# Routed expert tokens in 8 expert lists instead of 28 pair lists, with tiles of 512 rows stored split and loaded transposed

## The reference

```
x = x + conv_part(layernorm over channels(x))
    # conv_part: per image and channel a 3x3 depthwise convolution whose 9 taps are a softmax of
    # linear maps of the channel means and maxima, plus a bias, plus its own input
t = tokens(x)                                # 32768 tokens of 128 channels
n = layernorm(t)
logits = n @ Wg + bg                         # 8 experts
top 2 of the 8, weights = softmax over the 2
t = t + sum over the 2 chosen e of  w_e * (gelu(n @ W1[e] + b1[e]) @ W2[e] + b2[e])     # H = 512
return images(t)
```

## Time and profile before

| | |
|---|---|
| median of 3 runs | 1804.54 us (1803.85 to 1805.2) |
| span of the profiled execution | 1798.2 us |
| TensorE busy | 1536.5 us, 85% |
| VectorE busy | 1396.4 us, 78% |
| ScalarE busy | 1202.0 us, 67% |
| GpSimd busy | 866.1 us, 48% |
| moved by DMA | 115.76 MB |

### The profile page before, as it was taken

How to read it: one execution, slowest core, us unless ns; L and a number is a source line. 1 busy time by engine, 2 the same in 40 slices (tenths; PEclk the granted TensorE clock), 3 DMA queues, 4 the chain that set the end, 5 groups by cost and what they waited for, 6 DMA issues and landing times.

```text
span 1798.2 us, 45758 instructions
## 1 busy us (share of the span) xinstructions
PE 1536.5 (85%) x12335; PEld 1186.0 (66%) x12336; DVE 1396.4 (78%) x2440; ACT 1202.0 (67%) x2949; POOL 866.1 (48%) x905
## 2 busy tenths in 40 slices
PE   5889999999999519999999999999999999999665
PEld 2445555555555307878888778878777788878555
DVE  0468888788788737888888888888888888888644
ACT  3466667767666308878777887788777887888400
POOL 1003455355355464555555555555555555555500
PEclk8899999999998659999999999999999999999965
DMA  3211121121121061111111111111111111110099
GB/s 120 59 35 56 54 72 59 59 70 60 61 58 49 31 146 30 39 39 36 42 42 37 36 38 39 39 40 35 41 42 37 40 38 42 42 37 22 22 374 359
DMA packets 90626, 115.76 MB, mean 64 GB/s; under 512 B 15286, under 2 KB 71794, under 8 KB 90583
## 3 DMA queue, kind: packets, MB, share of 16 engines
q1 hardware_dynamic: 65784, 62.29, 12.2%
q0 software_dynamic: 18176, 34.27, 5.5%
q10 hardware_dynamic: 6624, 18.69, 2.8%
HBM read 60.22 MB, written 58.61 MB: 66 GB/s over the span
## 4 chain that ended last, share of the span: by engine, by line
issue 31%; POOL 28%; PE 24%; ACT 7%; DMA 4%; DVE 4%; POOLq 1%; SPq 0%; ACTq 0%; DVEq 0%
POOL token_out L454 12%; POOL yt L449 9%; PE psV L731 8%; POOL yt L447 6%; DMA ye<-token_out 4%; PE psR L703 3%; PE psV L691 3%; ACT spent L531 2%; PE psA L682 2%; PE psT L716 2%; PE psR L747 2%; PE psG L718 1%; POOL rows_by_pair L439 1%; DVE x L963 1%; ACT sq L508 1%
## 5 line engine op out<-in xcount | busy, mean ns | idle before, releaser
L1138 DVE TENSOR_TENSOR gl<-g,gh 128x1024 f16<-128x1024 f32 x312 | 438.1, 1404 | 70.5 <-ACT gh L624 65.2
L439 POOL DMA_INDIRECT rows_by_pair<-rows,idx x256 | 265.0, 1035 | 393.3 <-issue 245.4
L454 POOL DMA_INDIRECT token_out<-yt,rt x312 | 323.1, 1036 | 184.6 <-POOL yt L449 133.5
L616 ACT ACTIVATE g<-psV,b1col 128x256 f32<-128x256 f32 x624 | 244.4, 474 | 143.6 <-PE psV L825 143.6
L616 ACT ACTIVATE g<-psT,b1col 128x256 f32<-128x256 f32 x624 | 244.4, 474 | 53.4 <-PE psT L825 53.4
L731 PE MATMUL psV<-lp,diag 128*128 128x512 f32 x512 | 254.2, 626 | 24.8 <-ACT cv L524 14.6
L823 PE MATMUL psV<-xh,wall 128*128 128x256 f16 x624 | 171.9, 275 | 94.6 <-DVE xl L1128 53.8
L447 POOL TENSOR_TENSOR yt<-ya 128x256 f32<-128x256 f32 x156 | 112.9, 724 | 247.0 <-DVE ya L1150 246.9
L841 PE MATMUL psG<-wall,gh 128*128 x1248 | 222.7, 273 | 1.7 <-DVE ya L1146 1.4
L841 PE MATMUL psR<-wall,gh 128*128 x1248 | 222.7, 273 | 0.7 <-DVE ya L1150 0.7
L842 PE MATMUL psG<-wall,gl 128*128 x1248 | 214.3, 219 | 0.0
(11 more groups left out here) (187 smaller groups left out, 3254.9 us busy)
## 6 DMA issues: line engine op xcount, KB each, us to landing
rt<-rows_by_pair SPq DMA_DIRECT2D x156, 133.0 KB, 2.1
xb<-in_x_dram SPq DMA_DIRECT2D x32, 512.0 KB, 3.5
ye<-token_out SPq DMA_DIRECT2D x32, 512.0 KB, 9.1
out_dram<-oe ACTq DMA_DIRECT2D x32, 512.0 KB, 5.8
token_out<-yt,rt POOLq DMA_INDIRECT x312, 2.3
rows_by_pair<-rows,idx POOLq DMA_INDIRECT x256, 2.4
stage<-in_L_ffn_W_dram SPq DMA_DIRECT2D x1, 2048.0 KB, 12.3
rows_by_pair<-pad_rows SPq DMA_DIRECT2D x15, 133.0 KB, 5.2
```

What stands on the lines that cost most here:

```text
L439: gp.indirect_dma_start(rows_dram, bass.IndirectOffsetOnAxis(ap=idx[p][:, b:b + 1].bitcast(U32), axis=0), rows[p][:, b, :], None).then_inc ...
L454: gp.indirect_dma_start(y_dram, bass.IndirectOffsetOnAxis(ap=rt[r][:, b, ID:ID + 1].bitcast(U32), axis=0), yt[r][:, b, :], None, bounds_ch ...
L616: last = sc_.activation(g[side][:, s * T:(s + 1) * T], hbank[side][:, s * T:(s + 1) * T], ACT.Gelu, bias=b1col[:, bass.ds(e * HS + s, 1)], ...
L1138: v.tensor_tensor(gl[side][:, :], g[side][:, :], gh[side][:, :], ALU.subtract).then_inc(lo_done, 1)
```

## The change

- **Lists.** Each token goes to two of 8 lists, one for each chosen expert. The indicator has 8 columns. The second entry of a token comes from a second buffer, `twin`, into which a DMA on SP's queue copies the row. GpSimd writes 32 times 128 rows in a unit. A row has 130 words: the token, its target row and its weight.
- **Split and normalised in stage A.** ScalarE normalises a token when it is turned (8 activations for an image, in place of the one copy in `keep`) and rounds it to float16, and VectorE forms the low part. The rows are stored as float16 high and low parts.
- **The convolution's result** is stored in HBM by SP for the last addition, which moves to stage C.
- **Tiles** have 512 rows of one expert: 136 tiles, in a ring of four. SP loads them transposed, so there is neither normalising, turning nor splitting in stage B; target rows and weights come with a second small load.
- **Stage B.** The up product has 512 columns. The gelu, casts and rests are made slice by slice (two casts on ScalarE, two on VectorE). The down product is as before for one expert, over four blocks of 128 rows, two PSUM banks to a tile, two sets of banks in turn. ScalarE copies the side columns of the bank to SBUF, VectorE adds them to the others and multiplies by the weight. GpSimd only issues four indirect stores, to one row for each choice of a token.
- **Stage C** loads both choices of each image and the convolution's result (16 images of it are loaded at the start of stage B), turns both on TensorE and adds the three on VectorE.

The diff, cut to its core:

```diff
-    T = 2 * P
+    T = 4 * P
     TB = T // P
-    CAP = NTOK + 2 * T
-    OFF = [a * (2 * E - a - 1) // 2 for a in range(E - 1)]
-    NT = NTOK // T + NPAIR
+    CAP = NTOK + T
+    NT = 2 * NTOK // T + E
...
-    RING = 6
-    assert NT % RING == 0 and RING % 6 == 0
+    RING = 4
+    assert NT % RING == 0
...
+            def copy_rows(st_, stage, k):
+
+                p, blks = st_.slot(stage), slice(k * NBLK, (k + 1) * NBLK)
+                sp.wait_ge(low_ready, st_.count(stage, 2, k + 1))
+                sp.dma_start(twin[p][:, blks, 0:2 * XW], rows[p][:, blks, 0:2 * XW]).then_inc(twin_in[2 * p + k], 16)
...
             def load_rows(first, r):
-                sp.dma_start(rt[r][:, :, :], rows_dram[bass.ds(first, T), :].rearrange("(p b) f -> p b f", b=TB)).then_inc(row_in[r], 16)
+                src = rows_dram[bass.ds(first, T), :]
+                sp.dma_start_transpose(xt[r][:, :, :], src[:, 0:2 * XW].bitcast(F16)).then_inc(row_in[r], 16)
+                sp.dma_start(meta[r][:, :, :], src[:, ID:RW].rearrange("(b p) f -> p b f", p=P)).then_inc(row_in[r], 16)
...
+            for j in range(NX):
+                load_x1(j, j)
+
...
+            def load_e(n, j):
+                for k in range(2):
+                    src = y_v[n] if isinstance(n, int) else y_v[bass.ds(n, 1)].rearrange("a p k b d -> (a p) k b d")
+                    sp.dma_start(ye[j][:, k, :, :], src[:, k, :, :]).then_inc(ye_in[j], 16)
...
-                    for b in range(NB2):
-                        gp.indirect_dma_start(rows_dram, bass.IndirectOffsetOnAxis(ap=idx[p][:, b:b + 1].bitcast(U32), axis=0),
-                                              rows[p][:, b, :], None).then_inc(rows_out[2 * p + b // NBLK], 16)
+                    pool.wait_ge(low_ready, images)
+                    for k in range(2):
+                        for c, src in enumerate((rows[p], twin[p])):
+                            if c == 1:
+                                pool.wait_ge(s_const, 3)
+                                pool.wait_ge(twin_in[2 * p + k], copies)
+                            for b in range(k * NBLK, (k + 1) * NBLK):
+                                gp.indirect_dma_start(rows_dram, bass.IndirectOffsetOnAxis(ap=idx[p][:, c, b:b + 1].bitcast(U32), axis=0),
+                                                      src[:, b, :], None).then_inc(rows_out[2 * p + k], 16)
...
-                    pool.wait_ge(ya_done, 2 * (RING * t + r) + 4)
-                    gp.tensor_tensor(yt[r][:, :, :], ya[r][:, :, 0:D], ya[r][:, :, D:2 * D], ALU.add).then_inc(ysum_done, 1)
-                    pool.wait_ge(ysum_done, RING * t + r + 1)
-                    gp.tensor_tensor(yt[r][:, :, :], yt[r][:, :, :], rt[r][:, :, 0:D], ALU.add).then_inc(yt_done, 1)
...
+            def normalise(st_, k):
...
+                for b in range(NBLK):
+                    at = slice(k * NBLK + b, k * NBLK + b + 1)
+                    last = sc_.activation(nrm[k][:, b, :], psT[:, b * P:(b + 1) * P], ACT.Identity, bias=nmr[p][:, at], scale=rstd[p][:, at])
+                last.then_inc(normed, 1)
...
+            def side(j, q):
+
+                act.wait_ge(y_ready, j + 3)
+                act.wait_ge(ysum_done, j + 1)
+                sc_.activation(yside[q][:, :, :], yparts[q][:, :, 1, :], ACT.Copy).then_inc(side_done, 1)
...
+            def dstep(j, r, t):
+                more = not isinstance(j, int)
                 for s in range(HS):
...
+                    if more or j + 1 < NT:
+                        up(j + 1, (r + 1) % RING, s, t + (r + 1) // RING)
+                    if s == 1 and (more or j + 2 < NT):
+                        expert(j + 2, (r + 2) % RING)
+                    down(j, r, s)
...
+            def combine(j, r):
+
+                q = r % 2
+                dve.wait_ge(side_done, j + 1)
+                v.tensor_tensor(ysum[q][:, :, :], yparts[q][:, :, 0, :], yside[q][:, :, :], ALU.add).then_inc(ysum_done, 1)
+                dve.wait_ge(ysum_done, j + 3)
+                v.tensor_tensor(yt[r][:, :, :], ysum[q][:, :, :], meta[r][:, :, 1:2].broadcast_to([P, TB, D]), ALU.mult).then_inc(yt_done, 1)
...
+                    parts(RING * t + r + 1, (r + 1) % 2)
+                    combine(RING * t + r, r)
```

More of the change, by code:

```diff
@@ L209, in conv_moe_block @@
[L209 to L218, removed]
+        lg, lg2, eq, sc = (sb(n, [P, NB2, E]) for n in ("lg", "lg2", "eq", "sc"))
@@ L425, in _ @@
             images = pool.alloc_register("images")
+            copies = pool.alloc_register("copies")
             tiles = pool.alloc_register("tiles")
-            for reg in (routed, images, tiles):
+            for reg in (routed, images, copies):
                 pool.reg_mov(reg, 0)
             with pool.Fori(0, NU // 2, 1) as t:
+                pool.reg_alu(copies, copies, 16, ALU.add)
                 for p in range(2):
@@ L791, in _, with expert @@
             pe.wait_ge(idx_ready, NU)
-            off = [[pe.alloc_register(f"off{q}{side}") for side in range(2)] for q in range(3)]
-            def experts(j, q):
+            off = [pe.alloc_register(f"off{r}") for r in range(RING)]
+            def expert(j, r):
                 at = TW * j + T_OFF
-                pe.load(off[q], tab[0:1, at:at + 2] if isinstance(j, int) else tab[0:1, bass.ds(at, 2)])
-            def weights(q, side):
-                return pe.snap(off[q][side], min_val=0, max_val=(E - 1) * EW)
@@ new lines, in down @@
+            def down(j, r, s):
+                w, q = weights(r), r % 2
+                pe.wait_ge(lo_done, HS * (j + 2) + s + 1)
+                if s in ACT_CAST:
+                    pe.wait_ge(hi_act, len(ACT_CAST) * j + ACT_CAST.index(s) + 1)
+                if s == 0:
+                    pe.wait_ge(ysum_done, j + 1)
+                bank = ybank[q]
+                both = wall[:, bass.ds(w + (O_2 + 2 * s * D), 2 * D)]
+                high = wall[:, bass.ds(w + (O_2 + 2 * s * D), D)]
+                for b in range(TB):
+                    lhs = slice(b * P, (b + 1) * P)
+                    te.matmul(bank[:, 2 * b * D:2 * (b + 1) * D], gh[q][s][:, lhs], both, start=(s == 0 and b % 2 == 0), stop=False, skip_group_check=True)
+                    te.matmul(bank[:, 2 * b * D:(2 * b + 1) * D], gl[q][s][:, lhs], high, start=False, stop=False, skip_group_check=True)
+                if s == HS - 1:
+                    bias = wall[:, bass.ds(w + O_B2, D)]
+                    for b in range(TB):
+                        last = te.matmul(bank[:, 2 * b * D:(2 * b + 1) * D], bias_sel[:, :], bias, start=False, stop=(b % 2 == 1), skip_group_check=True)
+                    last.then_inc(y_ready, 1)
@@ L952, in add_image @@
                 dve.wait_ge(cv_ready, st_.count(2, 4, 2 * k + 2))
+                if not st_.fixed or st_.turns(2) > 0:
+                    dve.wait_ge(x1_out[j], 16 * st_.turns(2))
                 v.tensor_tensor(x1[j][:, :], cv[k][:, :], xb[j][:, :], ALU.add).then_inc(x_used, 1)
```

563 lines of the change are left out of this document (249 added, 314 removed).

## The result

The changed kernel takes **2060.94 us** (median of 4 runs, 2055.36 to 2073.14) against 1804.37 us for the kernel before: a ratio of 1.1435, 95% interval 1.1395 to 1.1474. The forecast was 1925 with a range of 1820 to 2065. The sign is right, the time lies just inside the upper edge of the range, and the loss of 257 us is twice the 120 that were forecast. The profiled execution has a span of 2056.0 us, 257.8 more than the one of the earlier trace rows.

What follows compares the result with a forecast made beforehand. The prediction took GpSimd's issuing to bound stage A, the turn of the four slots stage B and bytes stage C: 1798.2 + 176 + 5 - 131 + 70 = 1918 us, or 1925 against the median of the runs, range 1820 to 2065.

Steps and rivals of the forecast that it cites:

- Stage A, +176: Convolution and routing: GpSimd's 32 indirect DMAs, 42.4 us in a unit, become the bound; 176 us more, bounds +140 and +224.
- Stage B, the ring: Experts: with four slots, each reloaded only after its last store lands, the slot's turn sets the period; 131 us less.
- The middle terms (4.2, 3.9, 2.4): Stage B slot's turn, in us: down product's end to GpSimd's start, on to its fourth DMA, then to the next load.
- T = 5.33 + L/3: Stage B: the period of a tile from one slot's turn, L being the load's time; 6.5 us taken, between 6.2 and 8.4.
- 5.5 us of down product: Stage B: TensorE's term in the slot's turn, following the arrival of the next tile's rows.
- the clock down as a rival: Stage A: waiting under GpSimd halves TensorE's clock for half its work, 48 us a unit, kernel 2015 us; chance 10%.
- L = 3.5: Stage B: a tile's transposing load with its small second load takes 3.5 us, within 2.6 to 9.1.
- loads of up to 6.5 us: Stage B rival of a slow transposing load: 2038 us at L = 6, 2183 at 9.1; chance 20%, half inside the range.
- Stage C, +70: Last stage: bound by bytes, 58.7 MB at 360 GB/s take 163 us instead of 93.2.
- Between the stages, +5: From the last row DMA to stage B: bigger first tiles, low clock and 16 image loads add 5 us, from 0 to +15.

Runs made afterwards that it cites:

- e2: The kernel before, with each row store of stage A issued a second time to a scratch tensor: 1980.63 us, ratio 1.0978.
- e1: The changed kernel with a ring of 8 tile slots instead of 4: 1807.35 us, ratio 1.0024 to the kernel before.
- e4: The changed kernel with VectorE's sum and weighting of a tile moved ahead of the last quarter of the next tile's casts and rests: 2010.41 us.
- e10: The changed kernel with three filler matmuls before each wait for rows, and sum and weighting ahead of the next tile's last quarter of casts and rests: 1961.36 us.
- e8: The changed kernel with three filler matmuls of 512 columns per tile on TensorE before the wait for rows: 2021.27 us, ratio 1.1232.
- e6: The changed kernel with 8 slots and without stage C's 16 reloads of the convolution's result: 1785.32 us, against 1807 with the reloads.
- h1: The kernel before, keeping its pair lists, 256-row tiles and ring of six, with rows normalised and split in stage A and loaded transposed: 1773.95 us, ratio 0.9827.

## Why the prediction was right in sign and half the size

**Stage A, +176: right.** The unit is GpSimd's 32 issues, 43.2 us in the unit that starts at 297.82 and 42.9 on the mean, where I had 42.4; the first DMA starts at 167.1 and not 162. e2 shows 178 us from the issues alone.

**Stage B, the ring: right in its mechanism.** That a slot's turn and not an engine sets the period is shown from two sides: e1 takes it away and the whole loss goes, e4 and e10 shorten one term of it and win about a third of it for each tile. The middle terms (4.2, 3.9, 2.4) measured 4.17, 4.03, 2.36.

**Stage B, T = 5.33 + L/3: the step that failed.** The 5.33 holds "then 5.5 us of down product", the time of TensorE's step at the full clock, taken from the earlier trace rows, a stretch at clock 1.00. It measured 7.18 us in the changed kernel. At the full clock it measures 5.62, in e8 and e10 for all but a few steps, so 1.56 of it are the clock: 0.52 us for a tile, 71 us in stage B. The other 0.12, the overlap with the next step's first matmul, is worth 5 us. e8 bears the size out: its step is 1.38 shorter, which is 63 us; its stores are 0.17 longer, which takes 8 back; and its period is 0.31 shorter, 42 us, as the tiles without a wait keep the rest. I had written the clock down as a rival, and put it in the wrong stage: in stage A it did drop, to 0.83, and cost nothing, for it lay under GpSimd; in stage B, where the earlier trace rows show 1.00 and I expected TensorE to wait, I never asked what the wait does to the step behind it. I had also thought of the wait as spread evenly, 1 us to a tile. It comes as one wait in three tiles with a mean of 3.8 us. The Trainium skill ("TensorE: Matmul & The Clock Gate", HAM oscillation) says that repeated waits for data throttle the clock again and again; the traces of stage B agree, with 0.91 against 0.99 to 1.00 under fillers and slow steps behind 35 of 45 waits, and it was the rule to apply there.

**Stage B, L = 3.5: too low by 0.87**, 39 us. Issue to use is 4.37. The transposing load's own issue is 1.25 to 1.29 us on SP before the small load can be issued, where the plain one's is 0.57; I had taken only landing times of single loads. The transposing itself is not what makes it long: with a plain load it is still 3.62 to 3.82. The Trainium skill ("DMA: Bandwidth & Descriptors", Latency and other measured facts) gives 261 GB/s for such a transposing load, by which my estimate for L was 3.1; 256 KB at that rate are 1 us of the 4.37, so the rate is not what sets L here, and the rule could not have told it.

Together 71 + 5 + 39 = 115 of the 118 us; the stores' 4.03 for 3.9 adds 6, and the other two terms came out 3 us shorter.

**That the time still lies in the range is luck.** The room at its top was meant for a slow clock in stage A and for loads of up to 6.5 us. Neither came; the clock in stage B filled it.

**Stage C, +70: bytes, at a lower rate.** 58.7 MB took 179.5 us, 327 GB/s, instead of 163 us at the 360 of the earlier trace rows. e6 points to bytes as what sets it. h1's stage C moves the same bytes as before's and takes 99.4 us instead of 93.2. Why the rate differs stays open.

**Between the stages, +5:** -2.5 measured. The 16 image loads cost nothing there.

## What to carry to other kernels

Ahead of an engine sum, add up the turn of a buffer slot, from load to load, and divide it by the slots less the steps for which a tile is held; if that is longer than any engine's work for a tile, that turn sets the pace, and with another slot the same sum is divided by one more. Then ask how the wait will lie (evenly, or in one piece every few tiles), and price the work behind it at the lower clock, if that work is itself in the turn. A wait that costs the clock hides gains too: before a shorter load is judged to bring nothing, hold the clock up with spare matmuls and measure again.

## What the runs showed of the hardware that I had not expected

- 816 useless matmuls of 512 columns make this kernel faster: 1994.1 against 2060.94 us, with the granted clock at 1.00 instead of 0.91.
- The same plain load was worth nothing at a clock of 0.89 (2060.52 us) and 34 us at a clock of 0.99 to 1.00 (1986.96 against 2021.27).
- The length of a wait alone doesn't tell whether TensorE's clock falls behind it: 10 of the 45 waits in the changed kernel, of 2.12 to 4.01 us, left it up, and one of 2.32 us in e4 had a slow step behind it. Plain loads made the waits shorter and the slow steps more (43 of 44 instead of 35 of 45).
- A transposing load of 256 KB holds SP for 1.25 to 1.29 us, a plain one for 0.57, and with a small second load it is usable 4.28 to 4.49 us after its issue against 3.62 to 3.82, so transposing costs 0.55 to 0.66 us in all.
- An indirect DMA of 128 rows costs GpSimd 1.27 us at its fastest, 0.30 of it between two instructions; 512 of them back to back took 686.5 us in the changed kernel (167.1 to 853.6), 1.34 for one.
